# Summing eight experts' products and the tokens: on GpSimd alone, or on GpSimd and TensorE

## The reference, cut to what matters

```python
t = t + _L1_attn_ref(_ln_t(t), Wq, bq, Wk, bk, Wv, bv)
u = _ln_t(t)
router_probs = softmax(u @ router_w + router_b)        # 8 experts
top_p, top_i = top_k(router_probs, 2)
top_p = top_p / sum(top_p)
expert_out = einsum('bnd,edc->bnec', u, expert_w) + expert_b
t = t + einsum('bnk,bnkc->bnc', top_p, take_along_axis(expert_out, top_i))
x = t transposed back to (image, channel, 56, 56)
```

## Time and profile before

| what | us |
|---|---|
| median of 3 runs | 3060.19 (3059.83 to 3061.37) |
| the profiled execution | 3060.19 |
| its span, first to last instruction | 3058.4 |
| PE busy | 2487.7 (81%) |
| DVE busy | 2398.1 (78%) |
| ACT busy | 1653.4 (54%) |
| POOL busy | 276.3 (9%) |
| mean granted clock of TensorE | 0.870 of full speed |

### The profile page before, as it was taken

One profiled execution on the slowest core, in us unless ns is written; L12 is line 12 of the kernel. 1 busy time (PEld: TensorE's weight loads), 2 busy tenths in 40 slices (PEclk: granted clock), 3 DMA queues, 4 the chain that ended last, 5 costly groups with the idle time before them and its releaser, 6 DMA issues. The chain is left out here.

```text
span 3058.4 us, 48225 instructions
## 1 busy us (share of the span) xinstructions
PE 2487.7 (81%) x18582; PEld 993.0 (32%) x18582; DVE 2398.1 (78%) x4202; ACT 1653.4 (54%) x2170; POOL 276.3 (9%) x273
## 2 busy tenths in 40 slices
PE   1846467483359999999999999999999997777786
PEld 0423132231012222222222222222222225666664
DVE  4445546455889999999999999999999913888887
ACT  0233243335017777777777777777777794333332
POOL 0000000001000000000000000000000000545455
PEclk9978678785559999999999999999999996666667
DMA  5585665823200110211011101110110002122220
GB/s 130 117 193 159 170 171 152 204 81 138 85 1 1 54 54 33 80 54 54 1 54 54 54 1 54 54 54 1 54 54 22 1 22 74 64 83 77 75 84 21
DMA packets 55031, 220.95 MB, mean 72 GB/s; under 512 B 13479, under 2 KB 26403, under 8 KB 46115
## 3 DMA queue, kind: packets, MB, share of 16 engines
q1 hardware_dynamic: 53618, 214.40, 24.3%
q10 hardware_dynamic: 1200, 3.69, 0.3%
HBM read 81.67 MB, written 74.60 MB: 51 GB/s over the span
## 5 line engine op out<-in xcount | busy, mean ns | idle before, releaser
L1105 DVE TENSOR_REDUCE at_XM<-at_psX 128x1 f32<-128x448 f32 x2688 | 1552.0, 619 | 69.5 <-PE at_psX L985 41.7
L1055 ACT ACTIVATE at_PR<-at_psS 128x896 f32<-128x896 f32 x1344 | 1159.3, 915 | 371.0 <-PE at_psS L964 368.7
L1001 PE MATMUL at_psV<-at_PR,at_V 128*32 128x448 f32 x5376 | 645.2, 552 | 0.5 <-ACT at_PR L1055 0.5
L964 PE MATMUL at_psS<-at_US,at_KS 128*128 128x448 f16 x2688 | 630.8, 356 | 2.5 <-ACT at_PR L1055 0.9
L985 PE MATMUL at_psX<-at_KS,at_US 64*128 64x448 f16 x1344 | 501.9, 373 | 83.4 <-DVE at_XM L1105 76.7
L985 PE MATMUL at_psX<-at_KS,at_UH 64*128 64x448 f16 x1344 | 501.9, 373 | 0.0
L985 PEld LDWEIGHTS at_psX<-at_KS,at_US 64*128 64x128 f16 x1344 | 125.1, 93 | 751.9 <-DVE at_XM L1105 719.6
L964 PEld LDWEIGHTS at_psS<-at_US,at_KS 128*128 128x128 f16 x2688 | 205.1, 98 | 288.5 <-ACT at_PR L1055 140.4
L1380 POOL TENSOR_TENSOR fi_WE<-fi_WE 128x256 f32<-128x256 f32 (+1 forms) x224 | 212.8, 978 | 172.7 <-DVE fi_WE L1434 171.9
L365 PE MATMUL psA<-sb_stacks,sb_lhs 128*32 128x448 f32 x1568 | 170.8, 565 | 23.4 <-DMA sb_stacks<-sb_T 10.5
L1434 DVE TENSOR_TENSOR fi_WE<-fi_psE,fi_WT 128x512 f32<-128x512 f32 (+1 forms) x208 | 132.5, 665 | 43.6 <-PE fi_psE L1283 34.0
(11 more groups left out here) (186 smaller groups left out, 2058.4 us busy)
## 6 DMA issues: line engine op xcount, KB each, us to landing
sb_stacks<-sb_Xp SPq DMA_DIRECT2D x64, 496.8 KB, 11.9
sb_stacks<-sb_T SPq DMA_DIRECT2D x64, 443.0 KB, 8.0
sums<-at_O SPq DMA_DIRECT2D x16, 1568.0 KB, 6.3
fi_SUMS<-sums SPq DMA_DIRECT2D x16, 1568.0 KB, 6.6
at_KS<-key_stacks SPq DMA_DIRECT2D x16, 784.0 KB, 7.8
at_US<-query_stacks SPq DMA_DIRECT2D x16, 784.0 KB, 9.8
key_stacks<-sb_KS SPq DMA_DIRECT2D x13, 784.0 KB, 4.9
query_stacks<-sb_YU SPq DMA_DIRECT2D x13, 784.0 KB, 3.6
```

The lines of the kernel that those rows point to most:

```text
L964: last = nc.tensor.matmul(psS[:, i % 2, j, 0:TILE], KS[:, b, c * P:(c + 1) * P], US[:, b, t * TILE:(t + 1) * TILE], start=True, stop=True)
L1001: last = nc.tensor.matmul(psV[C * q:C * q + C, 0:TILE], V[:, b, G * k + q, :], PR[:, (2 * q4 + q // 2) % PRS, q % 2, :], start=(k == 0), s ...
L1055: nc.scalar.activation(PR[:, (i - 2) % PRS], psS[:, i % 2, :, 0:TILE], ACT.Exp).then_inc(p_ready, 1)
L1105: nc.vector.tensor_reduce(o, psX[:, (at + j) % 3, 0:TILE], AX.X, ALU.max).then_inc(x_done, 1)
```

## The change

After the two folds POOL now folds a third time, two experts' tiles to one, and adds the tile of T1. `sums` then turns one tile per set instead of three, with a transpose in place of the three accumulated matmuls. POOL's loop is two steps longer, so that each of the four operations of a set stands behind one of another set; `quarter_folded` and `expert_sum` are new semaphores, and `folded` now follows the addition.

```diff
@@ -1293,11 +1293,9 @@
                     if s == 4 and (not isinstance(n, int) or n + 1 < N):
                         pe.wait_ge(lg_ready, n + 2)
                     w = min(G, NC - G * s) * C
-                    for e in range(E // 4 + 1):
-                        v = (WE[:, s, e] if e < E // 4 else T1[:, c, G * s:G * s + w // C]).rearrange("p q c -> p (q c)")
-                        last = nc.tensor.matmul(psB[0:w, s // 4, s % 4 * P:(s % 4 + 1) * P], v[:, 0:w], ident[:],
-                                                start=(e == 0), stop=(e == E // 4))
-                    last.then_inc(set_done, 1)
+                    v = WE[:, s, 0].rearrange("p q c -> p (q c)")
+                    nc.tensor.transpose(psB[0:w, s // 4, s % 4 * P:(s % 4 + 1) * P], v[:, 0:w], ident[:]).then_inc(
+                        set_done, 1)
 
             def step(n, c, r):
                 b = c % 2
@@ -1379,6 +1377,10 @@
                 w = min(G, NC - G * s)
                 return nc.gpsimd.tensor_tensor(WE[:, s, 0:h, 0:w], WE[:, s, 0:h, 0:w], WE[:, s, h:2 * h, 0:w], ALU.add)
 
+            def add_tokens(s, c):
+                w = min(G, NC - G * s)
+                return nc.gpsimd.tensor_tensor(WE[:, s, 0, 0:w], WE[:, s, 0, 0:w], T1[:, c, G * s:G * s + w], ALU.add)
+
             def residual(n, c, r):
                 b = c % 2
                 pool.wait_ge(o_done, n * 2 + 2)
@@ -1389,13 +1391,20 @@
                 b = c % 2
 
                 if beyond(n, 0):
-                    for s in range(QSETS + 1):
+                    first = n * QSETS - QSETS
+                    for s in range(QSETS + 3):
                         if s < QSETS:
                             pool.wait_ge(we_ready, n * NU - NU + min(2 * s + 2, NU))
                             fold(s, E // 2).then_inc(half_folded, 1)
-                        if s >= 1:
-                            pool.wait_ge(half_folded, n * QSETS - QSETS + s)
-                            fold(s - 1, E // 4).then_inc(folded, 1)
+                        if 1 <= s < QSETS + 1:
+                            pool.wait_ge(half_folded, first + s)
+                            fold(s - 1, E // 4).then_inc(quarter_folded, 1)
+                        if 2 <= s < QSETS + 2:
+                            pool.wait_ge(quarter_folded, first + s - 1)
+                            fold(s - 2, E // 8).then_inc(expert_sum, 1)
+                        if s >= 3:
+                            pool.wait_ge(expert_sum, first + s - 2)
+                            add_tokens(s - 3, (c - 1) % TURN).then_inc(folded, 1)
                 if not isinstance(n, int) or n + 1 < N:
                     residual(n + 1, (c + 1) % TURN, r + b)
```

More of the change, by code:

```diff
@@ L1186, in finish @@
         names = ("o_full o_done t1_ready t1_cen t1_sq t1_var t1_std xh_ready z_high z16_ready k_full zs_ready "
-                 "l_full lg_ready gap_ready gap_exp gates_ready e_full we_ready half_folded folded set_done out_ready order")
+                 "l_full lg_ready gap_ready gap_exp gates_ready e_full we_ready half_folded quarter_folded expert_sum folded set_done out_ready order")
         (o_full, o_done, t1_ready, t1_cen, t1_sq, t1_var, t1_std, xh_ready, z_high, z16_ready, k_full, zs_ready,
-         l_full, lg_ready, gap_ready, gap_exp, gates_ready, e_full, we_ready, half_folded, folded, set_done, out_ready,
+         l_full, lg_ready, gap_ready, gap_exp, gates_ready, e_full, we_ready, half_folded, quarter_folded, expert_sum, folded, set_done, out_ready,
          order) = map(sem, names.split())
```

## The result

| | before | after |
|---|---|---|
| median us | 3060.43 (4 runs) | 3079.47 (4 runs, 3078.82 to 3080.79) |
| ratio, 95% interval | | 1.0062 [1.0045, 1.008] |
| profiled execution, its span | 3060.19, 3058.4 | 3079.12, 3077.3 |
| mean granted clock | 0.870 | 0.852 |

What follows compares the result with a forecast made beforehand. The prediction took each turn's chain through DVE, with excursions to ACT and PE, as the bound. 3060.2 us plus 20.3 (fourteen turns), 1.2 (turn before the last image), 4.4 (last image) and 1 (clock) gave 3087, range 3068 to 3112.

Steps and rivals of the forecast that it cites:

- The largest term: Fourteen turns with folds and a `residual`: POOL's added work delays DVE by 1.45 us each, 20.3 us.
- What bounds the kernel, and that PE's saving lies beside the path: Last stage: a turn's chain runs through DVE with excursions to ACT and PE; `sums` is outside it, saving worth nothing.
- What comes onto POOL: POOL's queue: two more operations per full set, 5.5 us a turn; last add near 2859.1 us.
- What that does to DVE: Second expert, divide and gates: DVE operations with two SBUF inputs stall on POOL, turn grows 1.45 us, bounds 0 to 2.6.
- It no longer meets L1519 (-0.3 there) but L1522: End of the gates: `residual` stalls DVE's L1522 instead of L1519; L1522 ends at 2861.3 us instead of 2859.85.
- Up to L1496 nothing changes: DVE operations of the turn up to L1496 end no later; delays start with L1501, 0.54 us.
- What it does to PE's queue: `project` behind `sums` begins at 2859.4 us, takes 5.16 at the low clock; unit 2's products come at 2865.2.
- A tie, cost 0, at most 0.8: Unit 2's products at 2865.2 us against `weigh` wanting them at 2865.15: no cost, at most 0.8 us.
- The clock in the token stretch: From L1484 to the end of the last `weigh`: 1 us in the sum for PE's clock.
- the second rival: PE's clock always low: 0.25 us a turn, 0.8 more if `project` delays unit 2; 3101 us, chance 0.13.
- Full blocking: POOL and DVE fully block each other at the shared SBUF port: 2.3 us a turn, 3099 us, chance 0.22.
- signs of being wrong: Small POOL operations much over 0.46 us, L1464 waiting for `residual`, `weigh` waiting for unit 2, or turns of 30 us.

Runs made afterwards that it cites:

- The second experiment: Kernel before the change, with two more POOL operations per set of the added shapes on an unread scratch tile, `sums` as before: 3074.54 us, ratio 1.0036.
- the first experiment: Changed kernel, with PE running the first half of `project` after turning sets 0 to 2, ahead of sets 3 to 6: 3071.3 us, ratio 1.0033.

## Why the prediction was right, and where it was right by luck

The time (19 us for 26.9 forecast), its sign and its range were right. The largest term, 20.3 us for what POOL does to DVE, was not what happened, and one that I had put at nothing cost 10.8 us. That the total came out near is in good part luck.

- **What bounds the kernel, and that PE's saving lies beside the path**: right for the kernel before. Sums made with a fraction of the instructions brought nothing anywhere. What I did not see is that POOL's queue, once it has no gaps, itself sets the length of B and C.
- **What comes onto POOL**: right. `residual` at 4.89 us behind the gap for 4.76, the last image's queue 17.76 us for 17.6, the turn ahead of the last image and the last image together 5.8 us for 5.6 (1.2 and 4.4).
- **What that does to DVE**: wrong, in the step "It no longer meets L1519 (-0.3 there) but L1522". L1501 and L1505 were to end 0.54 and 0.82 us late. They ended 0.15 late, which is what the gap itself takes longer (0.34 us for 0.19): one started together with a fold and was the first through, the other just ahead of a fold's end. The old L1522 therefore started 4.32 us behind the gap and not 5.10, and the last operation of the gates was begun when `residual` came. C grew by 0.1 us a turn in the mean, and not by 1.45; what ends it is `residual`'s own result, for which the reduce waits. "Up to L1496 nothing changes" failed as well: the search for the first expert takes 3.3 us longer over the fourteen turns, with L1503 (the old L1494) at 1.32 us for 0.78. The second experiment has that very meeting, one operation further on, and there the term is 0.7 us.
- **What it does to PE's queue**: my working had the low clock, the start of `project` (2859.4, which is 5.1 us behind the gap; measured 2836.72 - 2831.54 = 5.2) and `weigh` of unit 2 at 10.9 us behind the gap (measured 11.06). Only the conclusion "A tie, cost 0, at most 0.8" failed, since DVE came earlier than in my sum and PE did not. It cost 10.8 us over 14 turns, shown by the first experiment; 11 of the turns have it. In the first, and in the two ahead of which DVE is held up by about 2 us at the loop's jump, A was 11.1 to 11.2 us as before. The turn's end was fixed by either path at nearly the same point, so an error in one was replaced by the other. Hence the right total with a wrong term.
- **The clock in the token stretch**: the 1 us in the sum did not come, nor the second rival's 0.25 us a turn. The stretch took 1.2 us less over the fourteen turns, at a clock of 0.68 against 0.64.
- **The rivals**: the second (the clock) is what happened, in its part about unit 2. Full blocking was not borne out: POOL's operations beside a DVE one with two SBUF inputs took 0.11 to 0.20 us more than alone (0.84 for 0.73, 0.57 for 0.46, 0.66 for 0.46), and `residual` ended 6.95 us behind the gap, where I had 6.76 and that rival 8.6.
- **The signs**: two of those that I had named as signs of being wrong came. `weigh` waited for unit 2, as the second rival says; and L1464 waited for `residual`, though without full blocking, because `residual` came late and DVE did not.

What stays open: which engine gets in first when two operations start together. L1510 did, and took no longer than alone; L1529, which also follows its predecessor at once and also starts together with a fold, did not, and took 0.47 us for 0.35, in all fourteen turns.

## What to carry to other kernels

Before giving work to an engine that is idle on average, look at what stands behind it in every queue: here a saving on TensorE turned into a later start of unrelated matmuls, at half the clock, because they were queued behind an operation that now waited for GpSimd. Moving them ahead of that wait cost nothing and recovered three quarters of what the turns had lost. And a long GpSimd operation beside a chain of short VectorE ones is priced by which of them it meets: half of the added work lengthened C by 5.6 us, all of it by 1.4, and splitting and placing `residual`, with no work taken away, shortened it by 7.7. Last, an engine that fills its gaps can start to set the pace though its busy share is low over the whole program (12% here); look at its idle time within the turn.

## What was not expected of the hardware

- When a VectorE and a GpSimd operation start together, either can be the one that waits: L1510 took 0.35 us and the fold beside it 0.66 for 0.46, while L1529 took 0.47 for 0.35 and the fold beside it 0.24, as alone.
- A TENSOR_SCALAR of 25 columns with one SBUF input waited for GpSimd as those with two do, 0.69 us for 0.17. The Trainium skill (SBUF — State Buffer, Who interferes with whom) has it that `tensor_scalar` can enter a mode that uses both ports and then contends with GpSimd; the run agrees.
- An operation of 200 columns that started 0.03 to 0.04 us ahead of `residual` lasted 0.37 us; one that started 0.07 us behind it lasted 2.04.
